# Splitting the additions of the mask's channel sums between VectorE, ScalarE and GpSimd in a group norm kernel

## What is computed

```python
x1 = g.sum(axis=1)                    # g = _gn(x, G=32)
m = x1 != 0
n = m.sum(axis=(1, 2)); Nmax = n.max()
...
inv = 1.0 / jnp.sqrt(var + EPS)       # per channel, over the masked pixels
out = jnp.where(m[:, None], g * inv[None, :, None, None], g)
return x + out
```

## Time and profile before

| | |
|---|---|
| median of 3 runs | 1299.51 us (1299.47 to 1301.48) |
| the profiled execution, its own time | 1300.32 us |
| its span, from first to last instruction | 1298.6 us |
| busy: VectorE, TensorE, ScalarE, GpSimd | 1044.2, 719.3, 614.4, 76.3 us |
| read and written in HBM | 268.44 MB each |

### The profile page before, as it was taken

One profiled execution on the slowest core, in us unless ns is written; L12 is line 12 of the kernel. 1 busy time (PEld: TensorE's weight loads), 2 busy tenths in 40 slices (PEclk: granted clock), 3 DMA queues, 4 the chain that ended last, 5 costly groups with the idle time before them and its releaser, 6 DMA issues.

```text
span 1298.6 us, 10016 instructions
## 1 busy us (share of the span) xinstructions
PE 719.3 (55%) x2882; PEld 319.2 (25%) x2882; DVE 1044.2 (80%) x2264; ACT 614.4 (47%) x578; POOL 76.3 (6%) x144
## 2 busy tenths in 40 slices
PE   0666644566444665446654466544666445654466
PEld 0223221222222222222222222222222122221222
DVE  7999787787787887878877878778798777877884
ACT  0555433555344553345533455434554335543455
POOL 0000000000000000000000000000000000000000
PEclk9988766877667876678766778667777678866777
DMA  9999999999999999999999999999999999999996
GB/s 380 414 421 420 421 421 420 422 421 421 420 421 421 420 421 421 421 421 421 420 421 420 422 421 420 421 418 414 420 419 409 421 421 420 400 421 418 414 401 270
DMA packets 135463, 537.54 MB, mean 414 GB/s; under 512 B 4336, under 2 KB 4336, under 8 KB 135408
## 3 DMA queue, kind: packets, MB, share of 16 engines
q1 hardware_dynamic: 69936, 276.83, 52.4%
q10 hardware_dynamic: 65472, 260.05, 48.8%
HBM read 268.44 MB, written 268.44 MB: 413 GB/s over the span
## 4 chain that ended last, share of the span: by engine, by line
DMA 61%; PE 20%; DVE 12%; ACT 4%; issue 2%; SPq 0%; DVEq 0%
DMA out_dram<-slots 40%; DMA slots<-in_x_dram 22%; PE flush L384 13%; DVE stats L434 5%; ACT slots L312 4%; PE stay L380 2%; PE stay L381 2%; DVE spread L417 2%; PE small_ps L350 1%; PE small_ps L360 1%; DVE sums L448 1%; DVE dev L493 1%; PE small_ps L361 1%; DVE sums L445 0%; DVE spread L467 0%
## 5 line engine op out<-in xcount | busy, mean ns | idle before, releaser
L434 DVE BATCH_NORM_STATS2 stats<-slots 128x6 f32<-128x512 f32 x1024 | 650.3, 680 | 160.3 <-DMA slots<-in_x_dram 158.9
L312 ACT ACTIVATE slots<-slots,out_bias,out_scale 128x1024 f32<-128x1024 f32 x512 | 594.7, 1230 | 148.3 <-PE flush L384 67.4
L384 PE MATMUL flush<-slots,weights 128*64 128x512 f32 x1536 | 423.1, 687 | 0.0
L448 DVE SCALAR_TENSOR_TENSOR sums<-flush,group_bias,sums 128x512 f32<-128x512 f32 x360 | 263.0, 738 | 43.6 <-PE flush L384 42.4
L384 PEld LDWEIGHTS flush<-slots,weights 128*64 128x64 f32 x1536 | 147.3, 156 | 216.0 <-issue 211.1
L324 ACT ACTIVATE by_image<-by_image,eps 128x16 f32<-128x16 f32 x32 | 9.8, 307 | 359.0 <-DVE by_image L471 359.0
L350 PE MATMUL small_ps<-stats,group_avg 128*128 128x64 f32 x64 | 22.0, 444 | 268.3 <-DVEq L460 268.3
L290 POOL TENSOR_TENSOR weights<-pair_sum,group_rstd 128x256 f32<-128x256 f32 (+1 forms) x128 | 73.2, 602 | 1157.8 <-DVE group_bias L484 1157.8
L380 PE MATMUL stay<-slots,weights 128*64 128x512 f32 x512 | 140.0, 604 | 0.0
L381 PE MATMUL stay<-minus_mean,weights 128*64 128x512 f32 x512 | 138.1, 593 | 0.0
L350 PE MATMUL small_ps<-spread,group_avg 128*128 128x64 f32 x64 | 22.1, 448 | 168.7 <-DVE spread L467 168.7
(11 more groups left out here) (51 smaller groups left out, 215.5 us busy)
## 6 DMA issues: line engine op xcount, KB each, us to landing
slots<-in_x_dram SPq DMA_DIRECT2D x127, 2048.0 KB, 18.0
out_dram<-slots ACTq DMA_DIRECT2D x124, 2048.0 KB, 32.4
out_dram<-slots SPq DMA_DIRECT2D x16, 512.0 KB, 5.0
slots<-in_x_dram SPq DMA_DIRECT2D x4, 512.0 KB, 14.1
```

The source lines that it names most:

```text
L312: nc.scalar.activation(out_in_ring(u, i), image_in_ring(u, i), ACT.Identity, bias=out_bias[:, u % 2, i:i + 1], scale=out_scale[:, u % 2, i ...
L384: nc.tensor.matmul(into, weight, source, start=True, stop=True).then_inc(image_summed, 1)
L434: last = V.bn_stats(stats[:, u % 2, k * BLOCK_STATS:(k + 1) * BLOCK_STATS], source)
L448: V.scalar_tensor_tensor(out=sums[:, at, :], in0=bank, scalar=share, in1=sums[:, at, :], op0=ALU.add, op1=ALU.add).then_inc(added, 1)
```

## The change

VectorE keeps six of a unit's twelve additions (images 0, 2, 5, 8, 10, 13, the list `by_dve`). For the other six (1, 4, 6, 9, 12, 14, the list `by_pool`) ScalarE reads the bank ahead of that image's `put_out`, adds `group_bias` and writes the result to one of three SBUF buffers, `fresh` (`take`); in unit 0 it writes straight to `sums`. GpSimd then adds `fresh` to `sums`. New semaphores `taken` and `added_by_pool` link them. TensorE waits for `taken` or `added`, whichever frees its bank. In unit 31 VectorE compares as before, and nothing is taken.

```diff
-    ADDS_BEFORE = {8: (0, 1, 2), 10: (3,), 12: (4,), 14: (5,), 16: (6, 7), 18: (8,), 20: (9,), 22: (10,), 24: (11,)}
+    by_dve = flushed[0::2]
+    by_pool = flushed[1::2]
+    ADDS_BEFORE = {8: by_dve[0:3], 14: by_dve[3:4], 16: by_dve[4:5], 20: by_dve[5:6]}
...
+        fresh = sb("fresh", [P, FRESH_BUFS, BLK])
...
+        def wait_for_bank(engine, u, i):
+            if u == LAST or i in by_dve:
+                engine.wait_ge(added, added_with(u, i))
+            else:
+                engine.wait_ge(taken, taken_with(u, i))
...
+                if 0 < u < LAST:
+                    for i in by_pool:
+                        n = taken_with(u - 1, i) - 1
+                        pool.wait_ge(taken, taken_with(u, i))
+                        if u > 1:
+                            pool.wait_ge(added_by_pool, taken_with(u - 2, i))
+                        into = sums[:, flushed.index(i), :]
+                        pool.tensor_tensor(into, fresh[:, n % FRESH_BUFS, :], into, ALU.add).then_inc(added_by_pool, 1)
...
+            def take(u, i):
+                if u == 0:
+                    into = sums[:, flushed.index(i), :]
+                else:
+                    n = taken_with(u - 1, i) - 1
+                    into = fresh[:, n % FRESH_BUFS, :]
+                    if n >= FRESH_BUFS:
+                        act.wait_ge(added_by_pool, n + 1 - FRESH_BUFS)
+                nc.scalar.activation(into, bank_of(u, i), ACT.Identity, bias=group_bias[:, u % 2, i:i + 1]).then_inc(taken, 1)
...
                     if u < LAST or i >= APART:
                         wait_for_sum(act, u, i)
+                    if u < LAST and i in by_pool:
+                        take(u, i)
                     put_out(u, i)
...
-                            pe.wait_ge(added, m + 1 - FLUSH_BANKS)
+                            before = (m - FLUSH_BANKS) // ADDS
+                            wait_for_bank(pe, before, flush_order(before)[(m - FLUSH_BANKS) % ADDS])
...
-                        for m in ADDS_BEFORE.get(k, ()):
-                            add_sums(u - 1, flushed[m])
+                        for i in ADDS_BEFORE.get(k, ()):
+                            add_sums(u - 1, i)
```

More of the change, by code:

```diff
@@ L20 @@
 RING = 10
+FRESH_BUFS = 3
 FLUSH_BANKS = 3
@@ L160, in norm_conv_kernel @@
         added = sem("added")
+        taken = sem("taken")
+        added_by_pool = sem("added_by_pool")
         out_ready = sem("out_ready")
@@ L201, in wait_for_sum, with bank_of, taken_with @@
             engine.wait_ge(image_summed, (u * B + sum_order(u).index(i) + 1) * BLOCKS)
+        def bank_of(u, i):
+            return flush[(u * ADDS + flush_order(u).index(i)) % FLUSH_BANKS][:, :]
         def added_with(u, i):
-            return u * ADDS + flush_order(u).index(i) + 1
+            return u * len(by_dve) + (flush_order(u) if u == LAST else by_dve).index(i) + 1
+        def taken_with(u, i):
+            return u * len(by_pool) + by_pool.index(i) + 1
+        def wait_for_bank(engine, u, i):
[3 more added lines that the diff above has]
+                engine.wait_ge(taken, taken_with(u, i))
         def wait_for_all_stores(engine):
@@ L441, in add_sums @@
                 at = flushed.index(i)
-                bank, share = flush[(added_with(u, i) - 1) % FLUSH_BANKS][:, :], group_bias[:, u % 2, i:i + 1]
+                share = group_bias[:, u % 2, i:i + 1]
                 wait_for_sum(dve, u, i)
                 if u == 0:
-                    V.tensor_scalar(sums[:, at, :], bank, share, None, ALU.add).then_inc(added, 1)
+                    V.tensor_scalar(sums[:, at, :], bank_of(u, i), share, None, ALU.add).then_inc(added, 1)
                 else:
                     dve.wait_ge(added, added_with(u - 1, i))
-                    V.scalar_tensor_tensor(out=sums[:, at, :], in0=bank, scalar=share, in1=sums[:, at, :],
+                    V.scalar_tensor_tensor(out=sums[:, at, :], in0=bank_of(u, i), scalar=share, in1=sums[:, at, :],
                                            op0=ALU.add, op1=ALU.add).then_inc(added, 1)
@@ L530, in count @@
                 else:
-                    bank = flush[(added_with(LAST, i) - 1) % FLUSH_BANKS][:, :]
-                    dve.wait_ge(added, added_with(LAST - 1, i))
-                    V.scalar_tensor_tensor(out=not_zero[:, i, :], in0=bank, scalar=group_bias[:, LAST % 2, i:i + 1],
+                    if i in by_dve:
+                        dve.wait_ge(added, added_with(LAST - 1, i))
+                    else:
+                        dve.wait_ge(added_by_pool, taken_with(LAST - 2, i))
+                    V.scalar_tensor_tensor(out=not_zero[:, i, :], in0=bank_of(LAST, i), scalar=group_bias[:, LAST % 2, i:i + 1],
                                            in1=sums[:, flushed.index(i), :], op0=ALU.subtract, op1=ALU.not_equal,
@@ L540, in _ @@
             dve.wait_ge(counted, len(kept))
-            dve.wait_ge(added, UNITS * ADDS)
+            dve.wait_ge(added, LAST * len(by_dve) + ADDS)
             V.tensor_reduce(n_row, n_part[:, :], AX_X, ALU.add).then_inc(small_in, 1)
```

## The result

| | before | after |
|---|---|---|
| median | 1299.89 us (1299.12 to 1301.48, 15 runs) | 1296.88 us (1296.56 to 1297.70, 15 runs) |
| profiled execution, own time / span | 1300.32 / 1298.6 us | 1296.76 / 1294.7 us |

The ratio of the times is 0.9976, with a 95% interval of 0.9969 to 0.9984: the change makes the kernel 3.0 us faster, 0.24%. "No change" was forecast. The time lies in the range given, 0.08 us above its low end, but the forecast itself is wrong. That the range holds it is luck: its low end was there for rival (a), which did not occur.

A forecast was written before the change was run, and what follows sets the result against it. The prediction took the DMA engines to bound the kernel. Middle 0 and tail 0 (or -1.2 where it shows) left the time at the median of three runs, 1299.5 us; range 1296.8 to 1303.5.

The forecast's parts named there:

- rival (a): Tail: the lag is no single engine's, so the end follows the outputs' start; 1298.3 us, floor 1297.0; chance 0.20.
- The middle: Middle of the run: DMA engines are the bound and all others have slack, so the change gains 0.
- The rate from 40 to 1260: DMA rate from 40 to 1260 us: still 419 GB/s after the change.
- rival (b): Stretches with all engines at work: less VectorE SBUF traffic lifts 419 to 421 GB/s; 5.8 us less, 1293.7; chance 0.06.
- The cover of the stores: A unit's output: 16 us of older stores outstanding hide later stores (first one 1.7 us later), which cost nothing.
- a share below 1.0: Sign: a DMA share below 1.0 anywhere before 1264 us would show the cover of the stores wrong.
- The tail: End of the run: one lagging DMA engine sets it, so outputs could start 6.5 us later or any amount earlier; 0.
- the forecast's own test: Tail sign: the reading of the lag is wrong if the span shrank as much as the outputs' start moved.
- VectorE in the tail: Unit 31's statistics: VectorE's last block ends at 1258.9 against 1260.1, 1.2 us earlier, hidden by the lagging DMA engine.
- The costs: Whole run: busy time of VectorE falls to about 907 us, ScalarE rises to 735, GpSimd to 274; none of it counts.
- rival (d): Each unit: slow takes stall TensorE, which falls back to its slower clock; 42 us against 40.5, 1340; chance 0.03.
- (c): Each unit: added SBUF traffic of taken images causes rate dips of 0.13 us, 4 us in all; 1303.5; chance 0.09.

The follow-up runs named there:

- one wait: The kernel before with one wait on `added` per unit instead of twelve, 330 VectorE instructions fewer and no work moved: 1297.50 us, ratio 0.9982.

## Why the prediction was wrong, point by point

**The middle: 0. This is the step that failed.** The forecast saw that the DMA engines bound the kernel, and that VectorE, ScalarE and GpSimd had slack: right. It then took the engines' time as given, bytes over rate. Its own reading of the tail said that one engine of sixteen finishes some 6 us late, and it never asked what makes that one late. The answer is in what else the engine carries: about 22 packets of VectorE instructions (2773/128), 0.95 us each. A load goes out only when the slowest part of a store is in, so the kernel goes at that engine's pace. The change took three of these packets away, and 3 x 0.95 is the gain. The rows for it were on the page (`q14 instruction: 31`) and in the timeline of SyncE's queue, where every sixth load is late although a unit has four.

**The rate from 40 to 1260.** Forecast 419, and 421 in rival (b), which had a chance of 0.06 and a gain of 5.8 us. The outcome is 420, half of that rival, and by another cause: no port is involved, since twelve idle increments undo it. The dip to 394 at 1200 was read as a possible SBUF effect. After the change that stretch is at 408, but also in a kernel that keeps all of VectorE's additions (one wait) the slices of 409 and 400 are at 421, and the lowest between 40 and 1200 us is 413. That the engine behind causes such dips, by holding back the next load, is the likelier reading; no run shows it.

**The cover of the stores.** Forecast: 16 us of older stores outstanding, so later stores are free. In the end it held for the time, but the picture was too simple. The stores go out at these times after TensorE's first sum of unit 30 (1233.02 before, 1231.04 after): 8.42, 12.95, 17.48 and 24.40 us before, 8.32, 13.99, 19.09 and 24.77 after. That is -0.1, +1.0, +1.6 and +0.4 us, where +1.7, +2.4, +3.8 and +1.1 was forecast; the takes fill time in which ScalarE stood idle, and its idle time ahead of the outputs fell from 148.3 us to 62.3:

```profile
L355 ACT ACTIVATE slots<-slots,out_bias,out_scale 128x1024 f32<-128x1024 f32 x512 | 604.3, 1235 | 62.3 <-PE flush L430 53.9
```

And the 16 us were the backlog of the slowest engine only. The other fifteen had little left. The queues of the kernel before from 1120 to 1122 us, packets, MB, share (`q1` carries loads, `q10` stores), where unit 27's first store had been issued at 1118.87:

```profile
q1 hardware_dynamic: 128, 0.52, 108.6%
q10 hardware_dynamic: 8, 0.03, 3.5%
```

Hardly a packet of a store moves there: the older ones are through on nearly all engines. Loads alone fill the share at 0.52 MB in 2 us, since some of their packets take longer. This is not so of loads as such, as the windows of the same kernel show, the first from its start, where there are only loads:

```profile
5.00:20.00 15.00, 0.00 (x0) 0.00 (x0) 10.87 (x18) 0.00 (x0) 0.00 (x0) 1.00 1.03 412
1120.00:1122.00 2.00, 2.00 (x12) 0.89 (x11) 2.00 (x4) 2.00 (x2) 0.00 (x0) 1.00 1.12 276
1122.00:1124.00 2.00, 2.00 (x12) 0.89 (x9) 2.00 (x4) 2.00 (x3) 0.00 (x0) 1.00 0.88 313
```

Why packets are slow at 1120 is open. The forecast took a share below 1.0 as the sign of a broken cover. The share does fall, to 0.88 from 1122 to 1124, already in the kernel before, but the clearer sign is the rate, 339 GB/s from 1116 to 1124.

**The tail: 0.** Right, and for the reason given: starts of the outputs from 1267.15 to 1271.25 leave the span at 1298.6 or 1298.7, and the lagging engine is seen alone until 1276.8. Rival (a) falls with it. The cover is 5.3 us instead of 6.5. In the changed kernel the span shrank by 3.9 and the outputs moved by 3.33, which by the forecast's own test would have spoken for the rival; the test was poor, since whatever makes the middle shorter moves both.

**VectorE in the tail.** Forecast 1.2 us earlier. Counted from TensorE's first sum of unit 30, the last block ends at 27.08 us before and 25.73 after: 1.35 us earlier, by the mechanism described (the wait of 2.70 us ahead of image 5's addition).

**The costs.** A take is 677 ns (forecast 0.65 us), an addition on GpSimd 1277 ns (1.1; above both ends of 1.04 and 1.22). Busy times count overlapping instructions once. ScalarE's rose by 100.5 us for 186 takes, 0.54 each, where the forecast took 0.65 for the part that counts (715 instead of 735). VectorE's fell by 124 us for 186 additions, 0.67 each and not 0.738, and a block is unchanged at 680 ns (920 instead of 907). GpSimd's is 306 instead of 274, for the size of its addition. None of it counts. VectorE was not slowed beside GpSimd: its addition took 738 ns before and 740 after, its block 680 in both. TensorE was not slowed either, 719.7 us and a clock of 0.74 in the middle; rival (d) did not occur, nor did (c). The price of (d) was also added up wrongly: 42 us against 40.5 are 1.5 us a unit and not 1.3, so 1344.5 and not 1340.

## What to carry to other kernels

When a kernel is bound by DMA and one DMA engine of the sixteen finishes last, ask what that engine carries besides the data, and look at the spacing of the loads: a late step in a rhythm that is not the kernel's own points to it. Here the rhythm was the instruction stream of one compute engine, so taking waits and increments off that engine, though it was idle a fifth of the time, gained 2.4 us, where the change with its moved work gained 3.0. Judge a full DMA share together with the rate: a share of 1.12 went with 276 GB/s here, and one of 1.02 with 419 over the middle.

## What the runs showed of the hardware

- Instructions are fetched by DMA packets while the kernel runs, about 128 instructions in one of 8 KB on `q14` (VectorE, ScalarE, GpSimd), and TensorE's on `q8` in packets of 16 KB.
- VectorE's packets cost time here, 0.86 to 1.05 us each going down from 22 and 1.5 to 1.6 going up. 1364 more instructions on ScalarE, GpSimd or TensorE changed the time by less than 0.15%. The trace does not name the engine, but at 1293.9 one packet of instructions stands in the stream of the lagging engine, and in the kernel with twelve idle instructions one at 1268.6 does not. That it is VectorE's alone that stand there is an inference from this and from the times.
- A packet of instructions takes 0.31 us of an engine (1.9% of 16 engines in 1 us). In the tail, where the engine is alone, it sets the stream back by 0.65 us, since the two packets of data behind it take 0.34 us each and not 0.16. In the middle it sets the stores back by 0.95. Where the other 0.3 us come from is open.
- Two engines working in SBUF, GpSimd with two SBUF inputs and VectorE with one, did not slow each other's rows by more than the 2 ns above.
